# Layer 1's attention: the value matmuls of a head group moved behind its weights and score steps

## What is computed

```
q = x @ Wq.T
k = concat([x_text @ Wk.T, x @ Wk.T]);  v = concat([x_text @ Wv.T, x @ Wv.T])
scores = einsum('bhnd,bhkd->bhnk', q, k) / sqrt(d)
attn = concat([tanh(gate), softmax(scores[..., 1:])])
out = einsum('bhnk,bhkd->bhnd', attn, v)       # then bfloat16, a layer norm, @ Wp.T + bp
```

## Time and profile before

| | us |
|---|---|
| median of 3 runs | 1286.11 |
| lowest, highest | 1279.64, 1290.08 |
| the profiled execution, its own time | 1285.64 |
| its span | 1283.9 |
| granted TensorE clock over the span, mean share of full | 0.842 |
| TensorE busy | 977.4 (76%) |
| VectorE busy | 771.4 (60%) |
| ScalarE busy | 571.7 (45%) |

### The profile page before, as it was taken

One profiled execution on the slowest core, in us unless ns is written; L12 is line 12 of the kernel. 1 busy time (PEld: TensorE's weight loads), 2 busy tenths in 40 slices (PEclk: granted clock), 3 DMA queues, 4 the chain that ended last, 5 costly groups with the idle time before them and its releaser, 6 DMA issues. The chain is left out here.

```text
span 1283.9 us, 17163 instructions
## 1 busy us (share of the span) xinstructions
PE 977.4 (76%) x5366; PEld 731.0 (57%) x5366; DVE 771.4 (60%) x1924; ACT 571.7 (45%) x1101; POOL 393.6 (31%) x519
## 2 busy tenths in 40 slices
PE   2797576698888888488888888478867578883766
PEld 2575354566566665266666666357745357772544
DVE  3687565566766777366666656356765414545674
ACT  1575242355555555155555544156634133321553
POOL 2432002122323232146565656333310132210321
PEclk9899677667777778689999999689978679996887
DMA  4000000000000000000000000100000200000001
GB/s 117 1 2 2 1 1 19 1 18 18 18 18 18 18 9 10 1 1 1 1 1 1 1 1 1 36 1 2 2 19 1 64 2 1 1 1 1 1 1 33
DMA packets 25607, 14.12 MB, mean 11 GB/s; under 512 B 10776, under 2 KB 25007, under 8 KB 25391
## 3 DMA queue, kind: packets, MB, share of 16 engines
q1 hardware_dynamic: 25518, 13.03, 3.8%
HBM read 11.98 MB, written 1.05 MB: 10 GB/s over the span
## 5 line engine op out<-in xcount | busy, mean ns | idle before, releaser
L1470 POOL TENSOR_TENSOR L1f_h<-L1f_h,L1f_gb 128x512 f32<-128x512 f32 (+1 forms) x96 | 152.2, 1588 | 116.5 <-DVE L1f_h L1760 96.7
L718 ACT ACTIVATE L_pt<-bank 128x512 f32<-128x512 f32 x224 | 131.3, 597 | 60.8 <-PE bank L604 56.9
L705 ACT ACTIVATE L_part<-bank,L_bias_ca,const 128x256 fp32r<-128x256 f32 x128 | 68.9, 563 | 111.9 <-PE bank L545 111.9
L406 POOL TENSOR_TENSOR L_kc<-L_kc_all,const 128x256 fp32r<-128x256 f32 x96 | 59.0, 618 | 179.7 <-PE bank L604 127.1
L1760 DVE TENSOR_TENSOR L1f_h<-L1f_a,bank 128x512 f32<-128x512 f32 (+1 forms) x96 | 65.4, 682 | 69.9 <-ACT L1f_a L1600 69.3
L1600 ACT ACTIVATE L1f_a<-bank 128x512 f32<-128x512 f32 (+1 forms) x96 | 57.3, 597 | 111.9 <-PE bank L1525 111.8
L1768 DVE TENSOR_TENSOR L1f_h_lo<-L1f_h,L1f_h_hi 128x512 fp32r<-128x512 f32 (+1 forms) x96 | 88.2, 919 | 11.1 <-ACT L1f_h_hi L1613 11.1
L844 DVE TENSOR_REDUCE L_ms<-bank 128x2 f32<-128x512 f32 x128 | 84.5, 687 | 17.0 <-PE bank L566 16.7
L566 PE MATMUL bank<-L_k,L_q 32*128 32x256 f32 x256 | 73.4, 397 | 12.2 <-DVE L_ms L844 8.9
L830 DVE SCALAR_TENSOR_TENSOR L_q<-bank,L_bias_c,L_part 128x256 fp32r<-128x256 f32 x96 | 46.2, 481 | 58.9 <-ACT L_part L705 57.7
L842 DVE TENSOR_REDUCE L_mc<-bank 128x8 f32<-128x512 f32 (+1 forms) x96 | 65.4, 682 | 24.2 <-PE bank L559 14.8
(11 more groups left out here) (405 smaller groups left out, 2608.9 us busy)
## 6 DMA issues: line engine op xcount, KB each, us to landing
L_raw<-in_L_ffn_w_dram SPq DMA_DIRECT2D x8, 176.0 KB, 2.3
L_raw<-in_L_ffn_v_dram SPq DMA_DIRECT2D x8, 176.0 KB, 2.5
const<-in_const_dram SPq DMA_DIRECT2D x1, 1036.0 KB, 5.0
x<-in_x_dram SPq DMA_DIRECT2D x2, 512.0 KB
L_raw<-in_L_ffn_w_dram SPq DMA_DIRECT2D x8, 128.0 KB, 2.6
L_mask<-in_mask_Bx1xSxS_ff_dram SPq DMA_DIRECT2D x2, 512.0 KB
out_dram<-x SPq DMA_DIRECT2D x2, 512.0 KB
L_raw<-in_L_ffn_w_dram SPq DMA_DIRECT2D x8, 48.0 KB, 2.5
```

What stands on the lines that cost most here:

```text
L705: last = act.activation(part[:, i].bitcast(F32R), b_proj[:, i * S:(i + 1) * S], ACT.Identity, bias=bias_ca[:, i, g:g + 1], scale=pr.c("ak" ...
L718: act.activation(pt[:, g // 2, (g % 2) * NS + i], b_st[(g * NS + i) % 2][:], ACT.Exp, scale=scale).then_inc(sem["exp_done"], 1)
L1470: pool.tensor_tensor(h[0:m, r], h[0:m, r], gb[0:m, gate_slot(c)], ALU.mult).then_inc(sem["h_done"], 1)
```

## The change

In layer 1 (`own_keys`) the value rounds of a group are no longer dealt between its weights and score steps but follow them all, ahead of the group's end. Layers 0 and 2 keep their order. No instruction is added or removed; two more lines in the file move every line below by 3.

```diff
--- before.py
+++ after.py
@@ -303,7 +303,10 @@
                     steps += [("proj", *at), ("keys", *at)]
                 for at in group(g + 1):
                     steps += [("maxima", *at)]
-                steps += mixed(banks("weights", b, g), ahead[1:], pv[g]) + end[g]
+                if own_keys:
+                    steps += mixed(banks("weights", b, g), ahead[1:]) + pv[g] + end[g]
+                else:
+                    steps += mixed(banks("weights", b, g), ahead[1:], pv[g]) + end[g]
             return steps
 
         flush = [("pv", B - 1, 1, i) for i in range(NS)] + [("o_turn", B - 1), ("o_norm", B - 1), ("o_scale", B - 1), ("on_turn", B - 1),
```

## The result

| | us |
|---|---|
| before, median of 4 runs (lowest, highest) | 1282.88 (1269.41, 1290.08) |
| changed, median of 4 runs (lowest, highest) | 1323.38 (1321.86, 1328.75) |
| ratio | 1.0323, 95% interval 1.0281 to 1.0364 |
| profiled execution, changed | 1321.86 |

The sign and the lost cover were forecast, the size was not: +1.6% stood against +3.2%, because the forecast had the clock wrong where it mattered. The median lies at the very end of the range of 1290 to 1324, and the ratio times my 1286.11 lies beyond it, at 1328.

The account below looks back on a forecast made before the run. A loop over TensorE, ScalarE and VectorE was taken to bound layer 1's groups. Groups of three 6.9, groups of two 10.6 and copies 3.5 gave +21 us on 1286.11: 1307 us, +1.6%, range 1290 to 1324.

Parts of the forecast that it names:

- The cover: Value rounds ahead of s3 lie in TensorE's wait for VectorE's reduction of s1; 0.53 us of wait remains at full clock.
- The prices at either clock: A group from s1 to its end: 4.38 us at half clock, 4.29 at full without rounds, plus its block.
- The weights of the prices: Layer 1's attention: half-clock share 0.56, full 0.44, giving +0.86 us per group of three and +0.76 per group of two.
- The clock as a rival: Layer 1's groups: longer wait ahead of s3 raises the half-clock share from 0.56 to 0.8; 1323 us, chance 0.15.
- The copy: Group 1: L648 waits 0.50 us for ScalarE's copy of a half's result; seven group 2s have it, +3.5 us.
- Groups with L654: Six group 2s: the block is covered by L654's wait for VectorE's L895; 0 us, ends -0.3 and +1.0 each.
- GpSimd: Its wait for a half's last round ends some 3 us later in group 1, with 1 to 4 to spare: 0.
- Faster, by fewer changes of shape: Layer 1: 75 separate rounds become 30 blocks, saving 45 changes and 28 us if TensorE bounds: 1257 us, chance 0.07.

Follow-up runs that it names:

- both waits filled: Changed order plus thirteen unused matmuls a group, seven ahead of w2 and six ahead of s3 (last batch the six alone): 1277.20 us, 0.9917 to before.
- the one run that covered it: Changed kernel with w4 moved behind the block, so that w4 covers ScalarE's copy: 1328.74 us, 1.0317 to the kernel before.
- the half change in groups 0 and 2: Kernel before with the change made in groups 0 and 2 alone (blocks of three rounds): 1297.22 us, 1.0103 to before.

## Why the prediction was right on the sign and wrong on the size

**The cover.** Right. The rounds ahead of s3 stood in TensorE's wait for VectorE, the block at the end stands in none, and moving it back ahead of s3 takes the loss away (0.9991).

**The prices at either clock.** Right to 0.02 us at full clock. With both waits filled, s1 to s3 takes 379.93 - 376.90 = 3.03 us and s3 to the block 1.27, where I had 3.03 and 1.26. A block of two takes 1.00 and one of three 1.43, exactly as estimated from half of the earlier trace rows. At half clock the changed kernel's block of two runs from 386.37 to 388.3, 1.9 against 1.86. One reading was too general: I let s3 follow s1 by 3.03 us everywhere at full clock. In four of the seven group 3s before it followed after 2.63 us, in six of the seven after the change after 3.02, so that these groups lost more than I had priced.

**The weights of the prices: the step that failed.** "With shares 0.56 and 0.44" applied the mean clock of the stretch to both orders and to every group. It compared a group at half clock with the same group at half clock, and one at full with one at full. What happened is that groups which stood at full clock before have their block at half clock after: before, only 27% of the value matmuls were at half clock, after, 81%. With these shares a group of three cost 0.73 x 4.70 + 0.27 x 6.36 = 5.15 us before, and 4.29 + 0.81 x 2.71 + 0.19 x 1.43 = 6.76 after: +1.61, not +0.86. A group of two goes from 4.66 to 5.99: +1.33, not +0.76. The sum becomes 8 x 1.61 + 14 x 1.33 + 3.5 = 35 us. This was worked out with the result known. The two traces give the groups themselves, as means from the start of s1 to the start of what follows the group, its wait included:

| groups | forecast, us | before | changed | difference | clock over the value matmuls, before and changed |
|---|---|---|---|---|---|
| seven group 0s | +0.86 | 4.66 | 6.92 | +2.26 | 0.97, 0.50 |
| batch 0's group 2 | +0.86 | 6.37 | 7.09 | +0.72 | 0.50, 0.50 |
| seven group 1s, with the copy | +1.26 | 5.25 | 6.65 | +1.40 | 0.64, 0.53 |
| seven group 3s | +0.76 | 4.23 | 6.03 | +1.80 | 0.98, 0.71 |
| six group 2s, ahead of L654 | 0 | 6.76 | 7.23 | +0.47 | 0.86, 0.52 |

Where the clock before was already low the forecast holds within 0.2 us. The group 0s and 3s, at full clock before, make up 17 of the 22 us by which the table exceeds the forecast. With 0.9 us in batch 0's two groups without rounds, the table adds up to 43 us, and the rest of the groups gave 3 back: 39.5.

**The clock as a rival.** I had it as a rival with 0.15, at 1323, by another road: more groups wholly at half clock, a share of 0.8, a mean falling to about 0.6. The mean fell to 0.67 only, which is a share of 0.66. That its 1323 is the measured median is luck. What happened is a shift in phase: full clock in the waits, half clock in the block behind them. I had computed a wait of 1.7 us (it came as two, 0.84 ahead of w2 and 0.95 ahead of s3), had seen one fall of the clock after a microsecond with TensorE 0.59 busy, and still priced the two apart. The Trainium skill, TensorE: Matmul & The Clock Gate, What's actually happening, says that activity releases the throttle and idleness restores it. The runs agree in the main: 0.67, 0.73 and 0.95 with no, one and both waits filled, and 0.77 with eight matmuls where nothing waits.

**The copy.** +3.4 us of waits, as said. As a term it was right; as a lever it was worth nothing in the one run that covered it.

**Groups with L654.** Nearly right. That wait is gone, and the six groups cost 0.47 us each, 2.8 in all, inside the ends of -0.3 and +1.0. In the half change in groups 0 and 2 they cost 1.65 each, and its total of 13 us agrees with my re-priced 8 x 1.61 only because other parts of the groups became shorter.

**GpSimd.** Right: L657 waited 0.9 us for L898 in the stretch, so the later start of its chain cost nothing that shows.

**Faster, by fewer changes of shape.** Wrong for this order, since VectorE is the bound at s3. But a block ahead of w1 is 1.6% faster than the rounds dealt out. The Trainium skill, TensorEngine Tiling (Array Packing), Key Properties, says that a change of tiling mode drains TensorE, which points that way; no run here separates that saving from the clock's.

## What to carry to other kernels

An instruction that fits into a wait of its own engine for another one is free; find which wait of the loop covers it before it is moved. In this kernel the block behind two waits was paid at half clock (81% of its matmuls), so take the price of a moved matmul from where the clock will be at its new place, not from the mean of the stretch. A short experiment tells it: fill the waits with unused matmuls, and put the same number where nothing waits as a control.

## What the runs showed that I had not expected

Unused matmuls can shorten a kernel: thirteen a group in two waits took 46 us (3.5%) off the changed kernel, and eight a group 0.8% off the one before. The other side of it: leaving out 48 of 80 value rounds of before gave only 10 us, while the clock of the stretch went from 0.72 to 0.60. And a mean clock says little by itself: the same 0.67 stood at 1285 us with the rounds covered and at 1323 without.
